# Splitting and turning the context by ScalarE, GpSimd and a transposing transfer instead of TensorE and VectorE

## The reference

```python
scores = jnp.einsum('bhsr,bhlr->bhsl', q_r, k_r)
attn = jax.nn.softmax(scores, axis=-1)
ctx_c = jnp.einsum('bhsl,bld->bhsd', attn, kv_r)      # the context: 64 columns per head
ctx_lat = jnp.einsum('bhsd,hkd->bhsk', ctx_c, w_kc_kv)
ctx = ctx_lat.transpose(0, 2, 1, 3).reshape(Bv, Sv, H * K)
return ctx @ Wo.T
```

## Time and profile before

| | us |
|---|---|
| median of 3 runs | 483.36 (479.97 to 485.5) |
| profiled execution | 481.19 |
| its span, first to last instruction | 479.4 |
| TensorE matmuls busy | 412.8 (86%) |
| VectorE busy | 369.4 (77%) |
| ScalarE busy | 288.5 (60%) |
| GpSimd busy | 256.8 (54%) |

### The profile page before, as it was taken

How to read it: one execution, slowest core, us unless ns; L and a number is a source line. 1 busy time by engine, 2 the same in 40 slices (tenths; PEclk the granted TensorE clock), 3 DMA queues, 4 the chain that set the end, 5 groups by cost and what they waited for, 6 DMA issues and landing times.

```text
span 479.4 us, 11498 instructions
## 1 busy us (share of the span) xinstructions
PE 412.8 (86%) x4416; PEld 310.4 (65%) x4416; DVE 369.4 (77%) x751; ACT 288.5 (60%) x643; POOL 256.8 (54%) x294
## 2 busy tenths in 40 slices
PE   3965699999987789889898898887878999999994
PEld 3435366458866566667666666665756777887773
DVE  4357595968679989888989799985756689988991
ACT  2688679786355566556655766646424555667650
POOL 3174510401345555556677768774452588798453
PEclk9996799999989999999999999988989999999998
DMA  8895003930236746766687655589103386767742
GB/s 268 263 340 117 1 1 102 363 137 1 89 66 128 107 99 131 144 123 112 106 129 151 127 89 70 80 208 189 31 35 88 85 233 176 186 170 202 200 45 31
DMA packets 104599, 62.60 MB, mean 131 GB/s; under 512 B 72032, under 2 KB 100704, under 8 KB 104352
## 3 DMA queue, kind: packets, MB, share of 16 engines
q1 hardware_dynamic: 99792, 56.69, 49.2%
q0 software_dynamic: 4224, 4.79, 5.8%
q10 hardware_dynamic: 528, 0.38, 0.3%
HBM read 40.27 MB, written 8.55 MB: 102 GB/s over the span
## 4 chain that ended last, share of the span: by engine, by line
PE 52%; DMA 12%; DVE 11%; ACT 10%; issue 6%; POOL 6%; SPq 1%; POOLq 0%; ACTq 0%; DVEq 0%
PE psum L2180 10%; PE psum L2196 7%; PE psum L1872 6%; DMA lw<-lw 5%; DMA y_sb<-lw 4%; DVE lw L1299 4%; ACT lw L977 4%; PE psum L1797 3%; PE psum L1993 2%; PE psum L2201 2%; PE psum L1939 2%; PE psum L1932 2%; PE psum L1957 2%; POOL lw L653 2%; DVE lw L1359 2%
## 5 line engine op out<-in xcount | busy, mean ns | idle before, releaser
L653 POOL TENSOR_TENSOR lw<-lw 128x512 f32<-128x512 f32 x48 | 67.3, 1406 | 49.9 <-DVE lw L1299 46.4
L977 ACT ACTIVATE lw<-psum,nmax 128x256 f32<-128x256 f32 x128 | 59.2, 470 | 30.7 <-DVE nmax L1354 29.2
L1872 PE MATMUL psum<-lp 128*128 128x256 f16 x576 | 71.9, 275 | 0.0
L1299 DVE TENSOR_TENSOR lw<-psum,lp 128x1024 f32<-128x1024 f32 x48 | 58.4, 1218 | 5.8 <-PE psum L1872 5.0
L1872 PEld LDWEIGHTS psum<-lp 128*128 128x128 f16 x576 | 53.5, 99 | 13.9 <-issue 7.7
L1089 ACT ACTIVATE lw<-psum,b1w 128x320 f16<-128x320 f32 x64 | 33.8, 528 | 37.8 <-PE psum L2180 37.5
L2180 PE MATMUL psum<-lw,se 128*128 128x320 f16 x384 | 55.4, 301 | 0.0
L984 ACT ACTIVATE lw<-lw 128x512 f16<-128x512 f32 x60 | 37.7, 630 | 28.0 <-DMA lw<-lw 19.1
L755 POOL DMA_INDIRECT out_x<-lw,tslot x24 | 43.6, 1815 | 18.4 <-DVE lw L1624 6.8
L714 POOL TENSOR_TENSOR lw<-lw 128x512 f16<-128x512 f32 x30 | 36.1, 1204 | 28.7 <-ACT lw L984 28.7
L2180 PEld LDWEIGHTS psum<-lw,se 128*128 128x128 f16 x384 | 36.8, 98 | 16.7 <-DVE lw L1599 1.3
(11 more groups left out here) (248 smaller groups left out, 959.9 us busy)
## 6 DMA issues: line engine op xcount, KB each, us to landing
se<-in_w SPq DMA_DIRECT2D x11, 1024.0 KB
se<-in_w SPq DMA_DIRECT2D x40, 128.0 KB
dispatch<-in_empty SPq DMA_DIRECT2D x4, 662.5 KB, 10.5
lp<-in_Wq SPq DMA_DIRECT2D x2, 1024.0 KB, 9.6
se<-in_WoT SPq DMA_DIRECT2D x1, 2048.0 KB, 12.7
lw<-dispatch SPq DMA_DIRECT2D x7, 265.0 KB, 7.1
lp<-in_w_kc_q SPq DMA_DIRECT2D x2, 768.0 KB, 9.9
lp<-in_rotq SPq DMA_DIRECT2D x1, 1536.0 KB, 15.1
```

The lines of the kernel that those rows point to most:

```text
L653: nc.gpsimd.tensor_tensor(rope[:, c % QT, :].rearrange("p (h s) -> p h s", h=2), straight, crossed[:, ::-1, :], ALU.add).then_inc(g_rope, 1)
L977: A_(e_sb[:, n % 2, st * S:(st + 1) * S], bank[3 + n % 2][:, st * S:(st + 1) * S], ACT.Exp, bias=nmax[:, n % 2, st:st + 1], accum_out=esum ...
L1299: V.tensor_tensor(t12[:, c % 2], tile_bank(c).unsqueeze(1).broadcast_to([P, 2, 2 * S]), rotq[:, c % QT], ALU.mult).then_inc(v_t1, 1)
L1872: ins = M(tile_bank(c)[:, half * S:(half + 1) * S], m1[w][:, kc, half, col:col + P], (yth, ytl)[a][:, kc, b * S:(b + 1) * S], start=(n == ...
```

## The change

For the groups 0 to 13 `cxn` is split first and turned afterwards. ScalarE copies it to fp16 (`context_high`, in the place of `ct_high`), GpSimd subtracts (`ct_low`, placed behind `exps_low(n+1)`), both into a free part of `y_sb`, and SyncE issues one transposing transfer of the two halves (`turned_context`, behind `turned_exps(4g+1)` and ahead of that head's weight piece) into `ct`, whose layout changes with it. `project(g-2)` waits for that transfer and moves in TensorE's list from the end of group `g-1` to group `g`, between `context(n-1)` and `latent(g+1)`. `turn_context`, `ct_high` and VectorE's `ct_low` stay for the groups 14 and 15 only. Latent no longer waits for `ct_low`. In the routing two semaphores are replaced by waits of VectorE's own chain (`link`); what is computed stays the same.

```diff
@@ -42,6 +42,7 @@
 NHD = NHB - G
+NGD = NGB - 2
 PIECES = 16
@@ -157,7 +158,7 @@
         cxn = w2([512])
-        ct = [w2([512], F16) for _ in range(2)]
+        ct = w2([1024], F16).rearrange("p (w st a s) -> p w st a s", w=2, st=TPB, a=2)
         nmax = sb("nmax", [P, 2, TPB])
...
@@ -349,6 +351,11 @@
             return (bank[5], bank[1])[n % 2]
+
+        def context_halves(g):
+
+            at = NT - 2 * TPB if g < (B - 1) * NG - 2 else 0
+            return y_sb[:, at:at + TPB, :].rearrange("p a b -> p (a b)").bitcast(F16)
@@ -514,9 +521,18 @@
+            def turned_context(g):
+
+                sp.wait_ge(g_ct, g + 1)
+                if g >= 1:
+                    sp.wait_ge(p_out, g)
+                sp.dma_start_transpose(ct.rearrange("p w st a s -> p (w st a) s"), context_halves(g)).then_inc(d_ct, 16)
+
             half = PIECES // 2
                 turned_exps(n)
+                if n % G == 1 and n > G:
+                    turned_context(n // G - 1)
                 if n < half:
@@ -714,6 +730,12 @@
+            def ct_low(g):
+
+                pool.wait_ge(a_ct, g + 1)
+                halves = context_halves(g)
+                nc.gpsimd.tensor_tensor(halves[:, 512:1024], cxn, halves[:, 0:512], ALU.subtract).then_inc(g_ct, 1)
+
             def route_steps(n):
@@ -729,6 +751,8 @@
                 exps_low(n + 1)
+                if g >= 1:
+                    ct_low(g - 1)
                 if g + 2 < NGB:
@@ -989,11 +1013,17 @@
+            def context_high(g):
+
+                act.wait_ge(v_norm, g + 1)
+                if g >= 1:
+                    act.wait_ge(d_ct, 16 * g)
+                A_(context_halves(g)[:, 0:512], cxn, ACT.Copy).then_inc(a_ct, 1)
+
             def ct_high(g):
-                act.wait_ge(p_ct, g + 1)
-                if g >= 1:
-                    act.wait_ge(p_out, g)
-                A_(ct[0], context_bank(g)[:, :], ACT.Copy).then_inc(a_ct, 1)
+                act.wait_ge(p_ct, g - NGD + 1)
+                act.wait_ge(p_out, g)
+                A_(ct[:, 0].rearrange("p st a s -> p (st a s)"), context_bank(g)[:, :], ACT.Copy).then_inc(a_ct, 1)
@@ -1049,7 +1079,7 @@
                 if g >= 1:
-                    ct_high(g - 1)
+                    context_high(g - 1)
                 route_steps(n + 2)
@@ -1373,15 +1403,18 @@
                 dve.wait_ge(p_cx, G * (g + 1))
-                if g >= 1:
-                    dve.wait_ge(p_ct, g)
+                if g > NGD:
+                    dve.wait_ge(p_ct, g - NGD)
+                elif g >= 1:
+                    dve.wait_ge(g_ct, g)
                 V.tensor_tensor(cxn.rearrange("p (a b) -> p a b", b=DC),
                 dve.wait_ge(a_ct, g + 1)
-                V.tensor_tensor(ct[1], context_bank(g)[:, :], ct[0], ALU.subtract).then_inc(v_ct, 1)
+                high, low = [ct[:, w].rearrange("p st a s -> p (st a s)") for w in range(2)]
+                V.tensor_tensor(low, context_bank(g)[:, :], high, ALU.subtract).then_inc(v_ct, 1)
@@ -1419,12 +1452,12 @@
-                    V.max_index(i8[:, t, :], v8[:, t, :], l).then_inc(v_best, 1)
+                    ins = V.max_index(i8[:, t, :], v8[:, t, :], l)
+                link(ins)
-                dve.wait_ge(v_best, TPB * (b + 1))
...
@@ -1533,8 +1564,6 @@
                     turn(QT * (g + 2) + 1)
-                if g >= 1:
-                    ct_low(g - 1)
                 route_steps(n + 2)
@@ -1922,8 +1951,6 @@
                     pe.wait_ge(v_qz, g)
-                if g >= 3:
-                    pe.wait_ge(v_ct, g - 2)
                 x, y = bank[1], bank[2]
@@ -1998,19 +2025,22 @@
                 pe.wait_ge(v_norm, g + 1)
-                pe.wait_ge(v_qz, min(g + 3, NGB))
+                pe.wait_ge(v_qz, NGB)
                 if g == NGB - 1:
                     for pair in range(2):
-                        ins = TR(context_bank(g)[:, pair * S + st * P:pair * S + (st + 1) * P],
+                        ins = TR(context_bank(g)[:, (2 * st + pair) * P:(2 * st + pair + 1) * P],
                                  cxn[:, st * S + pair * P:st * S + (pair + 1) * P], identf[:, :])
                 b = g // NG
-                pe.wait_ge(v_ct, g + 1)
+                if g < NGD:
+                    pe.wait_ge(d_ct, 16 * (g + 1))
+                else:
+                    pe.wait_ge(v_ct, g - NGD + 1)
                 if g % NG == 0 and b >= 1:
@@ -2018,7 +2048,7 @@
                             last = g % NG == NG - 1 and pair == 1 and (a, w) == PASSES[-1]
-                            ins = M(bank[7][:, st * S:(st + 1) * S], ct[a][:, pair * S + st * P:pair * S + (st + 1) * P],
+                            ins = M(bank[7][:, st * S:(st + 1) * S], ct[:, a, st, pair, :],
                                     nn[w][:, 2 * (g % NG) + pair, :], start=(first and st == 0), stop=last,
@@ -2090,6 +2120,8 @@
                     context(n - 1)
+                if g >= 2:
+                    project(g - 2)
                 route_steps(n)
@@ -2098,22 +2130,18 @@
                     queries(QT * (g + 2) + 1)
-                if g >= 1:
-                    turn_context(g - 1)
                 route_steps(n + 2)
                 context(n + 1)
-                if g >= 1:
-                    project(g - 1)
                 route_steps(n + 3)
                     pe.wait_ge(v_t1, QT * NGB)
-                    pe.wait_ge(v_ct, NGB - 1)
+                    pe.wait_ge(v_ct, 1)
                 for t in (TPB * b, TPB * b + 1):
@@ -2125,6 +2153,7 @@
             scores(NHD // 2 + 1)
+            project(NGB - 3)
             route_count(B - 2)
             turn_scores(NHD + 1)
```

More of the change, by code:

```diff
@@ L303, in program @@
         s_y3, g_row, p_yT3, a_yT3, p_lg = sem("s_y3"), sem("g_row"), sem("p_yT3"), sem("a_yT3"), sem("p_lg")
-        g_nb, v_best, v_cnt, s_rows = sem("g_nb"), sem("v_best"), sem("v_cnt"), sem("s_rows")
-        v_sel, d_sel, s_base = sem("v_sel"), sem("d_sel"), sem("s_base")
+        g_nb, v_cnt, s_rows = sem("g_nb"), sem("v_cnt"), sem("s_rows")
+        v_sel, d_sel = sem("v_sel"), sem("d_sel")
+        g_ct, d_ct = sem("g_ct"), sem("d_ct")
         s_el, a_el, s_oh, p_pos, s_idx, v_meta = sem("s_el"), sem("a_el"), sem("s_oh"), sem("p_pos"), sem("s_idx"), sem("v_meta")
@@ L1439, in route_sides @@
                                 ALU.subtract).then_inc(s_el, 1)
-                V.tensor_scalar(base[:, ts, :], idf[:, ts, :], float(CAP), spare[:, 0:1], ALU.mult, ALU.subtract)\
-                    .then_inc(s_base, 1)
+                link(V.tensor_scalar(base[:, ts, :], idf[:, ts, :], float(CAP), spare[:, 0:1], ALU.mult, ALU.subtract))
             def route_weights(b):
@@ L1476, in route_place @@
                 dve.wait_ge(v_cnt, 2 * b + 2)
-                dve.wait_ge(s_base, b + 1)
                 link(V.tensor_reduce(pos[:, ts, :], pr[:, ts, :, :], AX.X, ALU.add))
```

## The result

The changed kernel took 532.59 us (median of 4 runs, 530.97 to 533.6) against 482.46 (479.97 to 485.5) for the kernel before: ratio 1.103, 95% interval 1.096 to 1.111. The direction was as forecast; 50 us is more than three times the forecast's 15, and outside its range.

What follows compares the result with a forecast made beforehand. It took the loop of landing, context, latent, `qz_high`, exponentials and SyncE's queue as deciding in some groups, VectorE and the scores in others. 481.2 + 14.8 (loop) + 1.0 (tail) = 497.0 us; range 480 to 510 us.

Steps and rivals of the forecast that it cites:

- The loop: Attention loop, one `qz_high` to the next, through `ct_low`, SyncE's transfers, context, `project` and latent: 14.67 us with both pieces.
- VectorE's busy total: Sign in the trace after: VectorE's busy share falls, total about 361 us.
- Rival (a): Attention loop: late issues hide and VectorE's 8.3 us come back, giving 472.9 us; chance 0.15.
- rival (b): Attention loop: only short groups lengthen, `project` finding TensorE idle anyway; 479 to 484 us; chance 0.11.
- the clock as a rival at 0.12: TensorE loses its clock in half of 13 groups, perhaps 2 us each: +13; chance 0.12, with slow landings.
- (c): Attention loop much slower as TensorE loses its clock: 510 us, 515 with slow landings; chance 0.12, with slow landings.
- The bound of 15: VectorE's `exps_low` beside more GpSimd work: up to 1.1 us more a group, 0 to +15, taken 0.
- The late issue: SyncE's queue: transfers of heads 4g+2 and 4g+3 wait behind the context transfer, which cannot start before `ct_low` ends.
- The move of `project`: TensorE, between context(4g-1) and latent(g+1): 12 matmuls now on the loop, 1.32 us a group.
- The gain of the removed work: Groups 0 to 13: all the saving worth at most 8.3 us, if VectorE sets the period.
- The upper bound of 8.3 us: `ct_low` taken off VectorE, 0.59 us in each of 14 groups: 8.3 us.
- The estimate of 21.8 us: TensorE's turns removed, priced by the Trainium skill at 1.56 us a group: gain of a TensorE-bound loop, instead of 8.4.

Runs made afterwards that it cites:

- e3: Changed kernel with 24 filler matmuls of 128x128 a group on TensorE ahead of context products: 523.29 us, ratio 1.084.
- e1: Changed kernel, but SyncE issues the context transfer behind the transfer of head 4g+3 instead of 4g+1: 530.41 us, ratio 1.099.
- e7: Changed kernel with the context transfer behind that of head 4g+3 and `ct_low` behind `exps_low(4g+3)` on GpSimd: 511.1 us, ratio 1.055.
- e6: Kernel before, with only `project(g-2)` moved between `context(n-1)` and `latent(g+1)`: 502.64 us, ratio 1.041.
- e2: Changed kernel, but ScalarE makes `context_high` ahead of `qz_high(g+1)`: 495.37 us, ratio 1.027.
- e5: Changed kernel with `context_high` ahead of `qz_high(g+1)` and `project(g-1)` back at the end of the group: 481.65 us, ratio 0.998.
- e4: Changed kernel with `project(g-1)` back at the end of the group, `context_high` still late: 507.31 us, ratio 1.049.
- e8: Changed kernel with `context_high` ahead of `qz_high(g+1)` and `project(g-2)` behind `context(n)`: 502.59 us, ratio 1.040.

## Why the prediction was right in direction and wrong in size

One group of the changed kernel, `qz_high` at 188.07 to `qz_high` at 205.31, against the forecast's terms in us:

| term | forecast | measured |
|---|---|---|
| to `exps_high`, to the exponentials of 4g+3, these | 0.49 + 0.52 + 0.92 | 0.49 + 0.52 + 0.90 |
| `context_high` | 0.62 | 0.71 |
| `ct_low` | 1.16 | 1.65 |
| two transfers and two pieces on SyncE | 3.92 | 3.92 |
| transfer of 4g+3, issue to the context product | 3.06 | 3.25 |
| context of 4g+3 | 0.45 | 0.63 |
| `project` | 1.32 | 2.68 |
| latent and hand-over | 2.21 | 2.49 |
| sum | 14.67 | 17.24 |

The same over all 13 intervals, read off the times of the same instructions, with e3 beside it:

| term, us in 13 intervals | forecast | after | with filler (e3) |
|---|---|---|---|
| ScalarE, up to `ct_low` | 35.1 | 38.5 | 37.7 |
| `ct_low` | 15.1 | 17.7 | 17.8 |
| transfers and pieces on SyncE | 46.2 | 48.3 | 47.7 |
| transfer of 4g+3, issue to the context product | 39.8 | 44.8 | 54.0 |
| context of 4g+3 | 5.8 | 8.0 | 5.3 |
| `project` | 17.2 | 32.5 | 18.8 |
| latent and hand-over | 28.7 | 32.2 | 28.7 |
| sum | 187.9 | 222.0 | 210.0 |

**The loop: right; its length: short by 34 us.** ScalarE's late half, GpSimd, SyncE's wait, two transfers queued behind it, context, `project`, latent: every link is in the chain after, and in 12 of the 13 intervals TensorE stood idle for the transfer of 4g+3. The intervals of groups 10 to 12, without pieces, took 16.07, 16.68 and 14.81 us, not near 13.3. VectorE's busy total, forecast as 361 us, is 360.9. Rival (a) and rival (b) fell: the issue of head 4g+3 came 196.26 - 188.07 = 8.19 us behind `qz_high`, where (a) needed 6.4 to stay.

**The step that failed: the clock as a rival at 0.12 and not as a term.** I put it as half of the groups falling, at 2 us each, on top of the forecast. But the forecast itself left TensorE some 4 us idle in each group, and the earlier trace rows had shown what a 2.18 us wait does to the 12 matmuls behind it. The last three terms of the table, TensorE's, were forecast at the full clock and took 21.0 us more: 15.3 for `project`, 3.5 for latent, 2.2 for context, of the 34 us that the forecast lacks. 12 of the 13 groups paid, all but the one from 294.63 to 309.19, whose clock was 1.00 and whose `project` took 1.41 us; so even (c), at 510 to 515, was too small. The other 13 us are smaller mis-sizings: 5.0 for the landing (one transfer took 4.90 us), 3.4 for ScalarE, 2.6 for `ct_low`, 2.1 for SyncE's issues. These are TensorE's lines from 150 to 395 us, of after, and from 150 to 345, of before:

```profile
L2051 PE MATMUL psum<-lp,lw 128*128 128x256 f16 x180 | 37.6, 392 | 0.0
...
L1959 PE MATMUL psum<-lw,lp 64*64 64x256 f32 x112 | 18.5, 456 | 0.0
```

```profile
L2021 PE MATMUL psum<-lp,lw 128*128 128x256 f16 x180 | 22.1, 273 | 0.7 <-DVE lw L1384 0.7
...
L1932 PE MATMUL psum<-lw,lp 64*64 64x256 f32 x112 | 15.2, 389 | 0.0
```

That the waits cause it is shown by e3, which filled them: the three terms fell back to 52.8 us, where the forecast had 51.7. That run returned only 9.3 us, since its filler also delays the context product (199.98 us, where the landing at 199.67 would have let it start sooner).

**`ct_low`: mis-sized in some groups.** The forecast took contention with VectorE's `exps_low` as 0, since that would start 2 us before. Its own numbers say otherwise: 0.49 + 0.52 + 0.92 + 0.62 = 2.55 us behind the `qz_high` at 191.37 is 193.92, the very start of `exps_low` in the earlier trace rows. After, `exps_low` started at 190.62, just ahead of `ct_low`, behind a turn of the queries on VectorE (189.48 to 190.71); VectorE and GpSimd by time, of after:

```profile
190.62 0.68 DVE L1389 TENSOR_TENSOR lw<-lw 128x512 f16<-128x512 f32 x1
```

```profile
190.69 1.62 POOL L737 TENSOR_TENSOR y_sb<-lw,y_sb 128x512 f16<-128x512 f32 x1 [6.69 <-ACT y_sb L1021]
```

1.62 us instead of 1.16, in 5 of 14 groups: 5 x 0.46 = 2.3 us in all. The bound of 15 was for VectorE's side; here GpSimd paid. The Trainium skill ("SBUF — State Buffer", Who interferes with whom) says that a VectorE instruction with two SBUF inputs contends with a GpSimd one that reads SBUF. This trace agrees: in just these five groups `exps_low` began less than 0.1 us ahead of `ct_low`, and once, at 360.82, it began behind it and took 1.10 us instead of 0.68.

**One queue instead of two.** The late issue was put down to SyncE. e1 and e7 show that GpSimd carries it as well: the forecast named the rotation and `exps_low(4g+3)` behind `ct_low`, and gave them no price. With SyncE as late as it is they cost little, which e1 and e7 bear out (moving both is worth 21.5 us, moving SyncE's alone 2.2, and moving GpSimd's alone costs 39.5); as advice for mending the change ("issue the transfer later") the forecast would have misled.

**The move of `project`: right.** 17.2 forecast, 18.7 measured alone (e6), 13.7 from e2 to e5; 25.3 in the changed kernel (e4 against it), where `project` itself takes nearly twice as long. The move and the clock meet here: `project` stands right behind the waits.

**Costed at nothing: not refuted.** GpSimd's 16 us, 14 issues and 14 transfers are in e5, and it takes the time of the kernel before; if they cost something, the removed work gave as much back.

**The gain of the removed work: none to be seen.** The upper bound of 8.3 us, rival (a), does not show even where both late steps are mended. In e5 VectorE is busy 144.59 of 175 us and no engine is full; what sets its pace was not found. The estimate of 21.8 us rests on 390 ns for one 128x128 block of bf16, which the Trainium skill ("VectorE: DVE Perf Modes", The three transpose paths) gives for TensorE; this trace does not bear it out as a saving, since the four fp32 blocks took 0.60 us together and e5, without them, is not faster.

## What to carry to other kernels

When a step moves to another engine, ask for each in-order queue that will wait for it what stands behind that wait, and place the producer's instruction first: 0.62 us of ScalarE work in the wrong place cost 37 us here. Before moving a consumer, look at the buffer it frees, too (e8). Where the sum leaves TensorE waiting a few us in every round and a trace of the kernel shows the clock low behind such a wait, cost the matmuls behind those waits at the low clock in the sum itself: here that was 21 us of 49.

## What the runs showed of the hardware

Waits of 2.37, 0.74 and 1.04 us in a group of 17.24, with TensorE busy 10.84 of 15 us, went with a mean granted clock of 0.77 over those 15 us, where the earlier trace rows showed a fall behind one wait. Over the 13 intervals the clock was 0.80 to 0.89 in twelve and 1.00 in one, although a wait of 2.93 us stands in that one too, at 304.09: one wait alone does not tell which level follows. Matmuls on constants in those waits brought the run's clock from 0.901 to 0.951, and the time down by 1.7%. The same filler in a kernel with short waits left the clock of the run at 0.950 and cost 2.5%. A GpSimd subtraction of 128x512 took 1.62 us instead of 1.16 when VectorE's `exps_low` began just ahead of it.
